# A deeper lead for the split of turned probability tiles in a fused attention and expert layer

## The chip, the cores and the metric

The kernel runs on one core of a Trainium2 chip. The metric is device time in microseconds (us) of one execution. A verdict of faster or slower needs a difference of over 2%.

## The reference

`x` is 2048 tokens by 256. The layer is attention and then a mixture of experts, each between two layer normalisations with a residual. Only the attention is touched by the change:

```python
x = L0_attn_x                                     # (1, 2048, 256)
# _L0_attn_ref, 16 heads of 128; w = codes * repeat(scales, 32)
q = _mxfp4_matmul(x, wq_codes, wq_scales) + bq    # the same for k and v
scores = jnp.einsum('bqhd,bkhd->bhqk', q, k) / jnp.sqrt(jnp.float32(HEAD_DIM))
attn = jax.nn.softmax(scores, axis=-1)            # 2048 x 2048 per head
out = jnp.einsum('bhqk,bkhd->bqhd', attn, v).reshape(B, S, NUM_HEADS * HEAD_DIM)
return _mxfp4_matmul(out, wo_codes, wo_scales) + bo
...
x = x + _layernorm(_L0_attn_ref(_layernorm(x, axis=-1), ...), axis=-1)
x = x + _layernorm(_L0_ffn_ref(_layernorm(x, axis=-1), ...), axis=-1)   # router, 8 experts, top 2
```

## The kernel before

Every float32 product is made of three products of a reduced float32 type (fp32r): each operand is split in a high part (the rounded copy) and a low part (operand minus high part), and hi x hi, hi x lo and lo x hi are summed (`product3`, lines 488 to 490). So each tile of probabilities needs a copy, which ScalarE (ACT) makes, and a subtraction, which GpSimd (POOL) makes.

The attention goes head by head (16), and in a head by chunks of 512 queries (4, index j), so there are 64 chunks. A chunk has 16 key positions of 128 keys and, at the same time, four row tiles of 128 queries (index r). Body (h, j) of the loop does two things interleaved: scores, maxima and exponentials of the *next* chunk (row tile r, in two halves g of 1024 keys), and the value products of the chunk that is under way. Positions 4r to 4r+3 belong to row tile r. "Step r" below is the time from the start of the first exponential of row tile r to the start of the next row tile's; a chunk is steps 0, 1, 2, 3.

The way of a probability: TensorE (PE) makes a half row tile of scores in `ps_s` (`scores`; three pairs of banks), VectorE (DVE) takes its maximum (L1000) and the shift (L1006), ACT the exponential (`exps`, L791), DVE turns it in blocks of 32 x 32 (`turn`, L1013), the DMA queue of SP brings the blocks of 1024 keys (group g) in place with 16 transfers (`turn_blocks`, L301) once the value products of the chunk before have used up the same group of `pT`, ACT copies a tile of 128 keys to `pT_hi` (`probs_hi`, L802), POOL subtracts in place (`probs_lo`, L393), and PE multiplies it with the values into `ps_a` (`weighted_values`). `pT_hi` is a ring of RING = 4 tiles: copy k waits until product k-4 is done.

The order on each engine is written out by hand and runs in order. At position p PE does the value product of key p - PV_LAG (12), ACT and POOL do copy and subtraction of key p - HI_LAG (10); a negative key is one of the chunk before. Around them, in step order:

- PE, row tile 3: scores (3,0), products 12 and 13, scores (3,1), the projection of queries (`q_proj`, which waits for `out_lo`), products 14 and 15. Row tile 0: products 0 and 1, scores (0,0), product 2, output projection, scores (0,1), product 3. In row tiles 1 and 2: scores (r,0), product 4r, product 4r+1, scores (r,1), products 4r+2 and 4r+3, with other projections between.
- ACT, each row tile: copies at 4r, 4r+1, 4r+2, exponential (r,0), copy at 4r+3, exponential (r,1). In row tile 3 `out_hi` stands behind the copy at 12, `q_hi` behind the copy at 14 and ahead of the exponential. At j = 3 the four copies of the next head's keys (`k_hi`) come before position 0.
- DVE, each row tile: maximum (r,0), turn (r-1,1), other work (`add_out`, L1040, in r = 0 and 1; `out_lo`, L1017, in r = 3), maximum (r,1), shift, turn (r,0).
- POOL: the weights of a head are unpacked between subtractions: keys at j = 0 and output at j = 1, both ahead of position 8; queries at j = 2 and values at j = 3, both ahead of position 0.
- SP: the 16 transfers of group 0, the 16 of group 1, and weight loads between; the query weights are loaded behind group 1 of body j = 1.

Of the kernel before, what the change touches and what calls it, by code (L numbers as in the profile page):

```python
# [8 lines left out]
def sandwich_layer(nc, x, wq, sq, bq, wk, sk, bk, wv, sv, bv, wo, so, bo, wr, wg, wu, wd, out):  # L9
# [35 lines left out]
    PAIRS = 3  # L45
    USES = TPC * NG2
    PV_LAG = 12
    HI_LAG = 10
    LOADS = Q4 * Q4 * 16
    CHUNKS = H * NCH  # L50

# [1 line left out]
    with ctx:  # L53
# [147 lines left out]
        def key_at(h, j, pos, lag):  # L201

            if pos >= lag:
                return (h, j, pos - lag) if has(h, j) else None
            if not has(h, j, -1):
                return None
            return ((h, j - 1) if j else (h - 1, NCH - 1)) + (pos + KT - lag,)
# [149 lines left out]
        def _(pool):  # L357
# [8 lines left out]
            def weights(k, h, codes=codes, scales=scales):  # L366

                wait(pool, w_loaded[k], 16 * (NG + 1) * (h + 1))

                if not isinstance(h, int) or h > 0:  # L370
                    if k == "o":
                        wait(pool, "oproj_ready", 2 * NCH * h)
                        wait(pool, "vb_ready", h)
                    else:
                        wait(pool, {"k": "k_lo", "v": "v_ready", "q": "q_lo"}[k], NCH * h)
                pool.tensor_tensor(w_hi[k][:, :, :], codes[:, :, :], scales[:, :, :], ALU.mult)\
                    .then_inc(w_hi_done[k], 1)
                col = {"o": "v", "k": "k", "q": "q", "v": None}[k]
                if col:
                    pool.tensor_copy(bias_now[col][:, :], bias_all[col][:, bass.ds(h, 1)])  # L380
                wait(pool, w_hi_done[k], h + 1)
                pool.tensor_tensor(codes[:, :, :], codes[:, :, :], scales[:, :, :], ALU.mult)\  # L382
                    .then_inc(w_scaled[k], 1)
                wait(pool, w_scaled[k], h + 1)
                pool.tensor_tensor(w_lo[k][:, :, :], codes[:, :, :], full(w_hi[k][:, :, :]), ALU.subtract)\
                    .then_inc(w_ready[k], 1)
# [14 lines left out]
            def body(h):  # L401
                before, last = isinstance(h, int) and h < 0, isinstance(h, int) and h == H - 1
                after = isinstance(h, int) and h == H
                for j in chunks_of(h):
                    for pos in range(KT):
                        if not before and not after:
# [6 lines left out]
                            if j == 3 and pos == 0 and not last:  # L413
                                weights("v", h + 1)
                        key = key_at(h, j, pos, HI_LAG)
                        if key:
# [347 lines left out]
        def _(act):  # L764
# [74 lines left out]
            def body(h):  # L839
                for j in chunks_of(h):  # L840
# [5 lines left out]
                    def key(pos):  # L846

                        at = key_at(h, j, pos, HI_LAG)
                        if at:
# [422 lines left out]
```

## Time and profile before

| | |
|---|---|
| median of 3 runs | 2824.37 us (2823.85 to 2857.05) |
| the profiled execution's own time | 2834.33 us |
| its span, first to last instruction | 2832.5 us |
| busy: PE, DVE, POOL, ACT | 81%, 61%, 55%, 49% of the span |
| mean granted TensorE clock | 0.943 |
| value part, first to last ScalarE copy (L802) | 94.2 to 2549.6 us |

A row of the timeline has the start of a group of instructions in us from the start of the span, its length, the engine, the line, the operation and its tiles, and in brackets the idle time of the engine before it and what ended that. Matmuls are pipelined: a value product is recorded as three matmuls of about 0.4 us, which start 0.23 us apart at full clock.

### The profile page before, as it was taken

To read this page: it belongs to the slowest core of one execution; us is meant where nothing else is said; L and a number is where in the kernel's file an instruction comes from. 1 tells how busy PE (TensorE), PEld (TensorE's weight loads), DVE (VectorE), ACT (ScalarE), POOL (GpSimd) and SP (SyncE) were. 2 spreads that over 40 slices of the span, in tenths; PEclk is the share of its full clock that TensorE was granted. 3 is DMA by queue.
4 is the path that set the end of the run, shared out by engine and by line. 5 is a ranking of instruction groups with operands and counts; after the bars stand their busy time and mean duration, and the time that the engine had idled before them with its cause. 6 is when DMAs were issued, how large, how long until landed. Compare 5 with 4: busy or idle time off the path is not lost.

```text
span 2832.5 us, 36223 instructions
## 1 busy us (share of the span) xinstructions
PE 2300.4 (81%) x10540; PEld 1812.0 (64%) x10540; DVE 1730.0 (61%) x2335; ACT 1389.5 (49%) x2492; POOL 1546.7 (55%) x1376
## 2 busy tenths in 40 slices
PE   4878787878788887878787878878787878855998
PEld 3667575756667666757575666657566657644876
DVE  4666666657566666666675756666666657645443
ACT  2454454545454555555454545544554545433332
POOL 1455556656565555565565656555556655554433
PEclk8999999989999999999999999999999999977999
DMA  4445454445454454555454645445455455470000
GB/s 75 112 109 118 105 126 112 112 107 134 102 125 109 111 126 105 117 126 118 105 121 110 135 103 124 113 108 117 105 126 120 112 116 120 113 180 11 8 8 15
DMA packets 152845, 298.68 MB, mean 105 GB/s; under 512 B 44896, under 2 KB 87264, under 8 KB 152800
## 3 DMA queue, kind: packets, MB, share of 16 engines
q1 hardware_dynamic: 152800, 298.11, 46.0%
q8 instruction: 24, 0.39, 0.1%
q14 instruction: 21, 0.17, 0.0%
HBM read 27.43 MB, written 2.10 MB: 10 GB/s over the span
## 4 chain that ended last, share of the span: by engine, by line
issue 41%; POOL 37%; PE 13%; DVE 4%; SPq 3%; DMA 2%; ACT 1%; POOLq 1%; ACTq 0%; DVEq 0%
POOL pT L393 33%; PE ps_s L488 2%; PE ps_s L489 2%; PE ps_s L490 2%; SPq L301 2%; POOL codes L382 1%; DVE part_max L1000 1%; DMA acc<-in_L_attn_bo 1%; PE ps_a L488 1%; PE ps_a L747 1%; DVE probs L1013 1%; PE ps_a L490 1%; PE ps_a L489 1%; PE ps_a L749 1%; PE ps_a L750 1%
## 5 line engine op out<-in xcount | busy, mean ns | idle before, releaser
L393 POOL TENSOR_TENSOR pT<-pT,pT_hi 128x512 fp32r<-128x512 f32 x1024 | 1298.4, 1289 | 975.5 <-ACT pT_hi L802 974.5
L791 ACT ACTIVATE probs<-ps_s,shift 128x1024 f32<-128x1024 f32 x512 | 569.2, 1112 | 777.6 <-DVE shift L1006 777.6
L488 PE MATMUL ps_a<-pT_hi,v_hi 128*128 128x512 f32 x1024 | 449.7, 439 | 408.3 <-POOL pT L393 408.2
L1000 DVE TENSOR_REDUCE part_max<-ps_s 128x1 f32<-128x1024 f32 x512 | 619.2, 1209 | 262.3 <-PE ps_s L490 261.2
L1013 DVE STREAM_TRANSPOSE probs<-probs 128x1024 f32<-128x1024 f32 x512 | 632.2, 1235 | 195.5 <-ACT probs L791 195.5
L802 ACT ACTIVATE pT_hi<-pT 128x512 fp32r<-128x512 f32 x1024 | 606.1, 626 | 76.1 <-DMA pT<-probs 55.1
L488 PEld LDWEIGHTS ps_a<-pT_hi,v_hi 128*128 128x128 f32 x1024 | 196.5, 192 | 559.6 <-POOL pT L393 526.4
L488 PE MATMUL ps_s<-kT_hi,qT_hi 128*128 128x512 f32 x1024 | 419.1, 409 | 9.1 <-ACT probs L791 6.6
L489 PE MATMUL ps_s<-kT_lo,qT_hi 128*128 128x512 f32 x1024 | 416.4, 407 | 0.0
L490 PE MATMUL ps_s<-kT_hi,qT_lo 128*128 128x512 f32 x1024 | 413.1, 403 | 0.0
L489 PE MATMUL ps_a<-pT,v_hi 128*128 128x512 f32 x1024 | 409.0, 399 | 0.0
L490 PE MATMUL ps_a<-pT_hi,v_lo 128*128 128x512 f32 x1024 | 408.6, 399 | 0.0
L488 PEld LDWEIGHTS ps_s<-kT_hi,qT_hi 128*128 128x128 f32 x1024 | 202.6, 198 | 55.2 <-ACT probs L791 8.6
L490 PEld LDWEIGHTS ps_s<-kT_hi,qT_lo 128*128 128x128 f32 x1024 | 201.5, 197 | 46.6
L489 PEld LDWEIGHTS ps_s<-kT_lo,qT_hi 128*128 128x128 f32 x1024 | 201.8, 197 | 42.2
L490 PEld LDWEIGHTS ps_a<-pT_hi,v_lo 128*128 128x128 f32 x1024 | 196.3, 192 | 44.8
L489 PEld LDWEIGHTS ps_a<-pT,v_hi 128*128 128x128 f32 x1024 | 197.4, 193 | 26.0
L1040 DVE SCALAR_TENSOR_TENSOR acc<-ps_a,rinv,acc 128x256 f32<-128x256 f32 x256 | 107.9, 462 | 136.0 <-PE ps_a L490 136.0
L488 PE MATMUL ps_a<-w_v_hi,xT_hi 128*128 128x128 f32 x512 | 146.2, 286 | 34.7 <-DVE oT_lo L1017 32.9
L1061 DVE TENSOR_TENSOR v_lo<-ps_a,v_hi 128x512 fp32r<-128x512 f32 x64 | 44.2, 691 | 176.0 <-ACT v_hi L830 176.0
L490 PE MATMUL ps_a<-w_v_hi,xT_lo 128*128 128x128 f32 x512 | 148.6, 290 | 0.0
L489 PE MATMUL ps_a<-w_v_lo,xT_hi 128*128 128x128 f32 x512 | 148.3, 290 | 0.0
(159 smaller groups left out, 2915.9 us busy)
## 6 DMA issues: line engine op xcount, KB each, us to landing
pT<-probs SPq DMA_DIRECT2D x2048, 128.0 KB, 2.4
probs<-in_L_attn_x SPq DMA_DIRECT2D x4, 512.0 KB, 5.3
codes<-in_L_attn_wk_codes SPq DMA_DIRECT2D x16, 128.0 KB, 2.2
scales<-in_L_attn_wk_scales SPq DMA_DIRECT2D x64, 32.0 KB, 2.8
acc<-in_L_attn_bo SPq DMA_DIRECT2D x1, 2048.0 KB, 31.2
codes<-in_L_attn_wo_codes SPq DMA_DIRECT2D x16, 128.0 KB, 2.1
scales<-in_L_attn_wo_scales SPq DMA_DIRECT2D x64, 32.0 KB, 1.8
x<-in_L_attn_x SPq DMA_DIRECT2D x4, 512.0 KB, 7.5
```

What stands on the lines that cost most here:

```text
L301: sp.dma_start(full(pT[32 * b:32 * (b + 1), g, i, :, :]).rearrange("p t q -> p (t q)"), blocks(j, g)[32 * i:32 * (i + 1), b].rearrange("p ...
L382: pool.tensor_tensor(codes[:, :, :], codes[:, :, :], scales[:, :, :], ALU.mult)\
L393: pool.tensor_tensor(tile, full(tile), full(pT_hi[:, k % RING, :]).rearrange("p (i q) -> p i q", i=Q4), ALU.subtract).then_inc(sm["p_lo_do ...
L488: nc.tensor.matmul(dst, lhs_hi, rhs_hi, start=first, stop=False)
L489: nc.tensor.matmul(dst, lhs_hi, rhs_lo, start=False, stop=False)
L490: return nc.tensor.matmul(dst, lhs_lo, rhs_hi, start=False, stop=last)
L791: nc.scalar.activation(out, src, ACT.Exp, bias=shift[:, j % 2, r:r + 1], scale=SCALE, accum_out=sums[:, j % 2, r, g:g + 1])\
L802: nc.scalar.activation(pT_hi[:, k % RING, :].rearrange("p (i q) -> p i q", i=Q4), full(pT[:, g, :, t, :]), ACT.Copy).then_inc(sm["p_hi_don ...
L1000: V.tensor_reduce(part_max[:, j % 2, r, g:g + 1], ps_s[:, pair_of(j, NG2 * r + g), :], AX.X, ALU.max)\
L1013: V.transpose(tile, tile).then_inc(sm["p_turned"], 1)
L1040: ins = V.scalar_tensor_tensor(acc[:, t, :], ps_a[:, j % 2, a * D:(a + 1) * D], rinv[:, jp % 2, 2 * i + a:2 * i + a + 1], acc[:, t, :], AL ...
L1061: V.tensor_tensor(v_lo[:, rows, :].rearrange("p a d -> p (a d)"), ps_a[:, bank, :], full(v_hi[:, rows, :]).rearrange("p a d -> p (a d)"), ...
```

## The change

Copies (ACT) and subtractions (POOL) of the turned tiles are done at position p for key p - 8 instead of p - 10. PE's products stay at p - 12, so they are led by four positions in place of two. The ring of four tiles stays.

```diff
     PV_LAG = 12
-    HI_LAG = 10
+    HI_LAG = 8
     LOADS = Q4 * Q4 * 16
```

The instruction order of PE, DVE and SP is the same. On ScalarE, body j = 1 of head 0, from row tile 2 (L802 is a copy, L791 an exponential, L810 `out_hi`; the brackets name the semaphores waited for, `pT_loaded0` is the landing of group 0, `pv_done` the value products). Before:

```order
L802 ACTIVATE pT_hi<-pT 128x512 [waits pv_done] x2
L802 ACTIVATE pT_hi<-pT 128x512 [waits pv_done,pT_loaded0]
L791 ACTIVATE probs,sums<-ps_s,shift 128x8x4x32 [waits shift_ready]
L802 ACTIVATE pT_hi<-pT 128x512 [waits pv_done]
L791 ACTIVATE probs,sums<-ps_s,shift 128x8x4x32 [waits shift_ready]
L802 ACTIVATE pT_hi<-pT 128x512 [waits pv_done]
L810 ACTIVATE oT_hi<-ps_a 128x4x4x32 [waits pv_done]
```

Changed:

```order
L802 ACTIVATE pT_hi<-pT 128x512 [waits pv_done,pT_loaded0]
L802 ACTIVATE pT_hi<-pT 128x512 [waits pv_done] x2
L791 ACTIVATE probs,sums<-ps_s,shift 128x8x4x32 [waits shift_ready]
L802 ACTIVATE pT_hi<-pT 128x512 [waits pv_done]
L791 ACTIVATE probs,sums<-ps_s,shift 128x8x4x32 [waits shift_ready]
L802 ACTIVATE pT_hi<-pT 128x512 [waits pv_done]
L810 ACTIVATE oT_hi<-ps_a 128x4x4x32 [waits pv_done]
```

The kinds of instructions keep their places; the copy that waits for the group's landing is the first of three ahead of the exponential, not the last.

On GpSimd, head 0, from its first subtraction (L393; L376 to L385 unpack weights: `w_o` at j = 1, `w_q` at j = 2). Before:

```order
L393 TENSOR_TENSOR pT<-pT,pT_hi 128x4x128 [waits p_hi_done] x14
L376 TENSOR_TENSOR w_o_hi<-codes,scales 128x256 [waits w_o_loaded]
L380 COPY bias_now_v<-bias_v 128x1
L382 TENSOR_TENSOR codes<-codes,scales 128x256 [waits w_o_hi_done]
L385 TENSOR_TENSOR w_o_lo<-codes,w_o_hi 128x256 [waits w_o_scaled]
L393 TENSOR_TENSOR pT<-pT,pT_hi 128x4x128 [waits p_hi_done] x8
L376 TENSOR_TENSOR w_q_hi<-codes,scales 128x256 [waits q_lo,w_q_loaded]
```

Changed:

```order
L393 TENSOR_TENSOR pT<-pT,pT_hi 128x4x128 [waits p_hi_done] x16
L376 TENSOR_TENSOR w_o_hi<-codes,scales 128x256 [waits w_o_loaded]
L380 COPY bias_now_v<-bias_v 128x1
L382 TENSOR_TENSOR codes<-codes,scales 128x256 [waits w_o_hi_done]
L385 TENSOR_TENSOR w_o_lo<-codes,w_o_hi 128x256 [waits w_o_scaled]
L393 TENSOR_TENSOR pT<-pT,pT_hi 128x4x128 [waits p_hi_done] x8
L376 TENSOR_TENSOR w_q_hi<-codes,scales 128x256 [waits q_lo,w_q_loaded]
```

Two more tiles are subtracted ahead of each unpacking of weights: ahead of the query weights 24 tiles (a whole chunk and half the next) and not 22.

## Rows read from the trace of the kernel before

**Rows 1.** The page's costliest groups: line, engine, operation, busy and mean ns, idle before.

```profile
L393 POOL TENSOR_TENSOR pT<-pT,pT_hi 128x512 fp32r<-128x512 f32 x1024 | 1298.4, 1289 | 975.5 <-ACT pT_hi L802 974.5
...
L488 PE MATMUL ps_a<-pT_hi,v_hi 128*128 128x512 f32 x1024 | 449.7, 439 | 408.3 <-POOL pT L393 408.2
```

**Rows 2.** Timeline of ACT, a plain chunk (j = 3): exponentials, one copy, q_hi.

```profile
1283.21 1.12 ACT L791 ACTIVATE probs<-ps_s,shift 128x1024 f32<-128x1024 f32 x1 [5.05 <-DVE shift L1006]
...
1290.22 1.12 ACT L791 ACTIVATE probs<-ps_s,shift 128x1024 f32<-128x1024 f32 x1 [2.62 <-DVE shift L1006]
...
1294.28 0.63 ACT L802 ACTIVATE pT_hi<-pT 128x512 fp32r<-128x512 f32 x1 [0.20 <-DMA pT<-probs]
...
1297.23 1.12 ACT L791 ACTIVATE probs<-ps_s,shift 128x1024 f32<-128x1024 f32 x1 [2.31 <-DVE shift L1006]
...
1304.31 0.69 ACT L816 ACTIVATE qT_hi<-ps_a,bias_now_q 128x512 fp32r<-128x512 f32 x1 [2.21 <-PE ps_a L490]
1304.89 1.11 ACT L791 ACTIVATE probs<-ps_s,shift 128x1024 f32<-128x1024 f32 x1
...
1315.02 1.11 ACT L791 ACTIVATE probs<-ps_s,shift 128x1024 f32<-128x1024 f32 x1 [5.12 <-DVE shift L1006]
```

**Rows 3.** Timeline of PE in the same chunk, value products and q_proj.

```profile
1293.35 0.50 PE L488 MATMUL ps_a<-pT_hi,v_hi 128*128 128x512 f32 x1 [1.09 <-POOL pT L393]
...
1302.60 0.51 PE L488 MATMUL ps_a<-xT_hi,w_q_hi 128*128 128x512 f32 x1
...
1304.10 0.40 PE L488 MATMUL ps_a<-pT_hi,v_hi 128*128 128x512 f32 x1
...
1308.01 0.50 PE L488 MATMUL ps_a<-pT_hi,v_hi 128*128 128x512 f32 x1 [1.65 <-POOL pT L393]
```

**Rows 4.** Timeline of DVE in the same chunk.

```profile
1287.88 0.83 DVE L1040 SCALAR_TENSOR_TENSOR acc<-ps_a,rinv,acc 128x256 f32<-128x256 f32 x2
...
1291.45 1.25 DVE L1013 STREAM_TRANSPOSE probs<-probs 128x1024 f32<-128x1024 f32 x1 [1.27 <-ACT probs L791]
...
1295.72 1.22 DVE L1000 TENSOR_REDUCE part_max<-ps_s 128x1 f32<-128x1024 f32 x1 [0.77 <-PE ps_s L490]
1296.98 0.21 DVE L1006 TENSOR_SCALAR shift<-part_max 128x1 f32<-128x1 f32 x1
...
1301.89 0.65 DVE L1017 TENSOR_TENSOR oT_lo<-ps_a,oT_hi 128x512 fp32r<-128x512 f32 x1
```

**Rows 5.** Timeline of SP's queue: group 0 of that chunk.

```profile
1282.29 10.03 SPq L301 DMA_DIRECT2D pT<-probs  x16
```

**Rows 6.** Timeline of ACT, chunk j = 1, row tiles 2 and 3, then row tile 0.

```profile
1219.10 1.11 ACT L791 ACTIVATE probs<-ps_s,shift 128x1024 f32<-128x1024 f32 x1 [2.48 <-DVE shift L1006]
...
1229.32 1.11 ACT L791 ACTIVATE probs<-ps_s,shift 128x1024 f32<-128x1024 f32 x1
...
1246.81 1.12 ACT L791 ACTIVATE probs<-ps_s,shift 128x1024 f32<-128x1024 f32 x1 [12.71 <-DVE shift L1006]
```

**Rows 7.** Timelines of SP's queue, POOL and PE around the query weights.

```profile
1221.42 10.03 SPq L301 DMA_DIRECT2D pT<-probs  x16
...
1236.92 0.72 POOL L376 TENSOR_TENSOR w_q_hi<-codes,scales 128x256 fp32r<-128x256 f32 x1 [4.53 <-DMA scales<-in_L_attn_wq_scales]
...
1239.21 3.74 POOL L393 TENSOR_TENSOR pT<-pT,pT_hi 128x512 fp32r<-128x512 f32 x3
...
1240.52 0.79 PE L488 MATMUL ps_a<-pT_hi,v_hi 128*128 128x512 f32 x1 [5.74 <-POOL pT L393]
```

**Rows 8.** Windows: length, busy of PE, PEld, DVE, ACT, POOL, granted clock, DMA.

```profile
1240.00:1244.00 4.00, 3.48 (x11) 3.09 (x12) 0.51 (x2) 0.00 (x0) 2.94 (x3) 0.50 0.00 0
```

**Rows 9.** Timeline of ACT, row tile 3 of chunk j = 2.

```profile
1268.84 1.11 ACT L791 ACTIVATE probs<-ps_s,shift 128x1024 f32<-128x1024 f32 x1
```

**Rows 10.** Timeline of ACT, row tile 3 of chunk j = 0, then row tile 0.

```profile
1348.43 1.11 ACT L791 ACTIVATE probs<-ps_s,shift 128x1024 f32<-128x1024 f32 x1
...
1358.49 1.12 ACT L791 ACTIVATE probs<-ps_s,shift 128x1024 f32<-128x1024 f32 x1 [5.69 <-DVE shift L1006]
```

## The prediction

> **What bounds the kernel now.** I read the page's costliest groups first, then the timeline of one head engine by engine. In the groups, TensorE (PE) stands idle 408.2 us in all before value products, waiting for POOL's subtraction, and POOL stands idle 974.5 us waiting for ACT's copy [rows 1]. So POOL is not short of time; the copies come late. The timeline says why. ACT's exponentials open every step, and in a plain chunk (j = 3) they start at 1283.21, 1290.22, 1297.23, 1304.89 and 1315.02: steps of 7.01, 7.01, 7.66 and 10.13, together 31.81 us [rows 2]. The copy at position 4r+3 stands behind the exponential (r,0), and with a lead of two it feeds the product at 4(r+1)+1, which stands ahead of the scores (r+1,1), whose maximum the next exponential needs. That is a closed loop: exponential, copy, subtraction, product, scores, maximum, exponential. It shows as PE's stalls of 1.09 and 1.65 us behind POOL [rows 3] and as DVE's 0.77 us of idle time behind PE in step 1 [rows 4].
>
> **The change.** No instruction is added or removed; 1024 copies and 1024 subtractions come two positions earlier. The copy behind exponential (r,0) now feeds the product at 4(r+1)+3, behind the scores (r+1,1), so the loop is opened. What is late next, step by step:
>
> Step 1. Without the stall, DVE is next: an exponential, 1.27 us until the turn may start [rows 4], then turn, maximum, turn, maximum, shift with nothing between. In step 1 that chain holds 0.77 us of idle time, so it comes to 7.01 - 0.77 = 6.24 us. PE needs less: two half tiles of scores and four products are 24 matmuls, 0.23 us apart, 5.5 us. Gain 0.8 us in chunks 1, 2 and 3; in chunk 0 value projections fill PE, and I take none. Step 0 has `add_out` (0.83 us [rows 4]) in the same chain: 6.24 + 0.83 = 7.07 against 7.01 now, so DVE bounds it already. Gain nil.
>
> Step 2 gets worse. The copy at 14 now takes a tile whose ring place is free only when the product at position 14 itself is done, and on PE that product stands behind `q_proj`. `q_proj` starts at 1302.60 when `out_lo` (1301.89 + 0.65) is there, the product at 14 at 1304.10 [rows 3, 4]. `q_hi` followed the projection at 1304.31 [rows 2]. It will follow copy 14: 1304.10, two matmul starts of 0.23 and the last matmul of 0.40 give 1304.96, plus a copy slot of 0.52 (the estimate is a copy's 0.63 less the overlap of about 0.1 us with its successor) gives 1305.5. So `q_hi` and the exponential (3,0) come 1.2 us later in every chunk. Loss 1.2 us x 4. In chunk 1 the step is 10.22 us now [rows 6], with stalls behind POOL unpacking `w_o`; the two tiles more of lead cover them, and it becomes 7.66 + 1.2 = 8.9. Net gain there 1.3.
>
> Step 3. The three products at 15, 0 and 1 no longer wait. From `q_proj`'s end PE has four products, scores, a product, an output projection and scores, some 6.9 us, which falls short of DVE's chain with an `add_out`, 7.0 us from the exponential (3,0). 10.13 [rows 2] and 10.06 [rows 10] become 7.0: gain 3.1 in chunks 3 and 0. In chunk 2 (14.37 us, 1268.84 to 1283.21 [rows 9, 2]) the next head's keys are projected in between; their chain does not move, only the stall behind it does, one of the kind of [rows 3]. I estimate the end of the step 0.9 us earlier (just under the 1.09 us there), its start 1.2 later, gain 2.1.
>
> Step 3 of chunk 1 is the large one: 17.49 us, 1229.32 to 1246.81 [rows 6]. POOL reaches the query weights at position 0 of body 2 and waits for them until 1236.92; subtractions go on at 1239.21, PE had stood 5.74 us, and then ran at the half clock: 0.50 granted, the 1.2 GHz level [rows 7, 8]. Now POOL has finished keys 4 to 7 of that chunk before it stops, which feed PE's products 0 to 3, both half tiles of scores, and so the next exponential. This step becomes 7.0 too, gain 10.5. The weights arrive no earlier, though: POOL resumes 17.8 us after SP started group 1 (1221.42 to 1239.21 [rows 7]), so the first tile is subtracted 1.3 us later [rows 1], 19.0 us after group 1's start, which is about exponential (2,0). PE wants it 16.3 us after: exponential (0,0) at 15.9 (8.9 + 7.0), its scores ended 1.7 before, a product (0.7) and scores (1.4) behind them. PE stands some 2.7 us. From 19.0 it has two products and an output projection (2.1), scores (1.4) and the 1.7 to the exponential: 24.2, against 15.9 + 7.0 = 22.9. Loss 1.2, rounded down.
>
> The sum per head is 3 x 0.8 - 3 x 1.2 + 1.3 + 2 x 3.1 + 2.1 + 10.5 - 1.2 = 17.7 us. With 15.5 heads (the first and last chunks lack parts of it) that is 274 us. The profiled execution took 2834 us, so 2560; it stands 10 us over the median, so I say **2550 us**.
>
> **The clock after the new stall.** The row at hand is a stall of 5.74 us with a half clock behind it; stalls of 1.09 and 1.65 us do not come with a slower product behind them [rows 3]. A stall of 2.7 us is between, nearest to the second; I take full clock. The other end: about 4 us at half clock, 2 us of work lost, 16 times, +32 us, and as much again where it falls twice. The Trainium skill, "TensorE: Matmul & The Clock Gate", section on the HAM clock gate, speaks for the slower end: the default state is throttled and activity releases it. By that reading the sum would be 2582 to 2614.
>
> **Transfers.** The first copy of each group is due earlier, and it stands ahead of an exponential. For group 0 SP starts 0.92 us before the exponential (0,0) (1282.29 against 1283.21), and the copy that waited for the landing starts at 1294.28, 11.99 us after [rows 5, 2]. So the copies at 8, 9, 10 can start 11.07 us after exponential (0,0) and take 1.6: 12.7, while the exponential (2,0) is due at 7.01 + 6.24 = 13.25. It holds by 0.6 us. Group 1 starts when product 11 is done, about exponential (2,0), and lands 12 us on, with 15.9 us to the exponential that needs it (8.9 + 7.0). I cost both at nothing. If the cover is gone, each late us is paid in full.
>
> **Rivals.** (1) *The transfers become the bound.* For: the margin of 0.6 us. Against: their start moves with PE's products, which get earlier too. If group 0 comes 2.4 us late for every chunk (as far as the copies at 8 and 9 and a stretch of SP's weight loads could put it), 64 x 2.4 = 154 us: about 2700.
> (2) *The ring takes the gain and the loss stays: slower.* The copy of key k waits for product k - 4, and with HI_LAG 8 these are at the same position. ACT is tied to PE there, ahead of the exponential. If PE still waits for POOL as often, because copies cannot run ahead of the ring, nothing is gained and the 1.2 us of step 2 is paid 64 times: +77 us, 2901 on the median. It decides where copy 4r+2 ends after the shift is ready. After scores (r,1) PE does the product at 4r+2 (0.69 us, 0.2 us to the end of the last matmul, copy slot 0.5: 1.4 us), while maximum and shift take from 1295.72 to 1297.23, 1.5 us, and 0.2 us of drain [rows 4, 2]: it holds by 0.3 us in steps 0 and 1. A busy POOL could use that up.
> (3) *The waits only move.* The stall behind the query weights moves from position 2 to position 4 in full length, and the rest is DVE's: 2824.
> (4) *The clock* as above: 2550 + 50 = 2600.
>
> **Numbers.** Forecast 0.66, clock 0.06, transfers 0.11: faster 0.83. Waits that move: 0.07 within 2%. Ring: 0.10 slower by over 2%. (Two per cent, 56 us, is what a measurement of this kernel can tell from no change.) The range begins at 2480, where step 2 loses nothing (64 x 1.2 = 77 us, 2473), and goes to 2730, past the transfers' case; outside are the last two cases.
>
> **What would show it.** In the new profile: idle time of PE behind POOL under 100 us; steps of a plain chunk of 7.0, 6.2, 8.9 and 7.0 us; the copy ahead of `q_hi` waiting for PE; the first exponential of body 2 about 7 us behind its predecessor, and PE idle for about 2.7 us at the first product of the row tile after it; ACT's waits for a landing late in the gap before an exponential that waits for the shift. I am wrong if ACT goes from a landing or a product directly to the exponential (0,0), (1,0) or (2,0) with the shift long ready, or if PE still stands behind POOL for hundreds of us.

## The result: 8.7% faster

The changed kernel takes 2588.22 us (median of 4 runs, 2584.68 to 2592.03) against 2828.9 us before on the same chip; the ratio is 0.9131, with a 95% interval of 0.9068 to 0.9194. The prediction was 2550 us in a range of 2480 to 2730. The profiled execution has a span of 2584.8 us against 2832.5.

### The profile page after: what moved, and what is told of

Its sections match the earlier page's. It is cut to its first block, busy times and chain, and to the rows that moved or that the text cites. A ratio compares the mean times of both kernels' runs of the same rounds, so it can differ in the third digit from the quotient of the medians.

```text
span 2584.8 us, 36223 instructions
## 1 busy us (share of the span) xinstructions
PE 2257.8 (87%) x10540; PEld 1810.7 (70%) x10540; DVE 1709.4 (66%) x2335; ACT 1406.0 (54%) x2492; POOL 1548.0 (60%) x1376
## 4 chain that ended last, share of the span: by engine, by line
issue 39%; POOL 37%; PE 14%; DVE 4%; SPq 2%; DMA 2%; ACT 1%; POOLq 1%; DVEq 0%; ACTq 0%
POOL pT L393 33%; PE ps_s L488 3%; PE ps_s L490 2%; PE ps_s L489 2%; POOL codes L382 2%; DVE probs L1013 1%; SPq L301 1%; DVE part_max L1000 1%; DMA acc<-in_L_attn_bo 1%; PE ps_a L747 1%; PE ps_a L488 1%; PE ps_a L490 1%; PE ps_a L489 1%; PE ps_a L749 1%; PE ps_a L750 1%
## 5 line engine op out<-in xcount | busy, mean ns | idle before, releaser
L393 POOL TENSOR_TENSOR pT<-pT,pT_hi 128x512 fp32r<-128x512 f32 x1024 | 1299.3, 1291 | 781.3 <-ACT pT_hi L802 781.2
L802 ACT ACTIVATE pT_hi<-pT 128x512 fp32r<-128x512 f32 x1024 | 616.8, 627 | 443.3 <-PE ps_a L490 367.3
L791 ACT ACTIVATE probs<-ps_s,shift 128x1024 f32<-128x1024 f32 x512 | 569.2, 1112 | 337.6 <-DVE shift L1006 337.6
L488 PE MATMUL ps_a<-pT_hi,v_hi 128*128 128x512 f32 x1024 | 421.0, 411 | 75.0 <-POOL pT L393 75.0
L489 PE MATMUL ps_s<-kT_lo,qT_hi 128*128 128x512 f32 x1024 | 410.3, 401 | 0.0
L1047 DVE SCALAR_TENSOR_TENSOR qT_lo<-ps_a,bias_now_q,qT_hi 128x512 fp32r<-128x512 f32 x64 | 48.0, 751 | 177.8 <-ACT qT_hi L816 157.5
L488 PEld LDWEIGHTS ps_a<-w_v_hi,xT_hi 128*128 128x128 f32 x512 | 107.6, 210 | 69.9 <-issue 45.0
```

The lines of the kernel that those rows point to most:

```text
L393: pool.tensor_tensor(tile, full(tile), full(pT_hi[:, k % RING, :]).rearrange("p (i q) -> p i q", i=Q4), ALU.subtract).then_inc(sm["p_lo_do ...
L488: nc.tensor.matmul(dst, lhs_hi, rhs_hi, start=first, stop=False)
L489: nc.tensor.matmul(dst, lhs_hi, rhs_lo, start=False, stop=False)
L791: nc.scalar.activation(out, src, ACT.Exp, bias=shift[:, j % 2, r:r + 1], scale=SCALE, accum_out=sums[:, j % 2, r, g:g + 1])\
L802: nc.scalar.activation(pT_hi[:, k % RING, :].rearrange("p (i q) -> p i q", i=Q4), full(pT[:, g, :, t, :]), ACT.Copy).then_inc(sm["p_hi_don ...
L1047: V.scalar_tensor_tensor(qT_lo[:, :], ps_a[:, (j + 1) % 2, :], bias_now["q"][:, :], full(qT_hi[:, :]), ALU.add, ALU.subtract).then_inc(sm[ ...
```

## The profile after

The page's groups that answer to [rows 1], and one that was small before: line, engine, operation, busy and mean ns, idle before.

```profile
L393 POOL TENSOR_TENSOR pT<-pT,pT_hi 128x512 fp32r<-128x512 f32 x1024 | 1299.3, 1291 | 781.3 <-ACT pT_hi L802 781.2
L802 ACT ACTIVATE pT_hi<-pT 128x512 fp32r<-128x512 f32 x1024 | 616.8, 627 | 443.3 <-PE ps_a L490 367.3
...
L488 PE MATMUL ps_a<-pT_hi,v_hi 128*128 128x512 f32 x1024 | 421.0, 411 | 75.0 <-POOL pT L393 75.0
```

PE's idle time behind POOL has gone from 408.2 to 75.0 us. In its place ACT waits 367.3 us for PE before copies: that is the ring, and it costs only where an exponential is queued behind the copy and the shift is ready.

A plain chunk (j = 3), timeline of ACT, to set beside [rows 2]:

```profile
1293.19 1.12 ACT L791 ACTIVATE probs<-ps_s,shift 128x1024 f32<-128x1024 f32 x1 [3.31 <-DVE shift L1006]
...
1300.10 1.12 ACT L791 ACTIVATE probs<-ps_s,shift 128x1024 f32<-128x1024 f32 x1 [1.95 <-DVE shift L1006]
...
1304.00 1.67 ACT L802 ACTIVATE pT_hi<-pT 128x512 fp32r<-128x512 f32 x3 [1.08 <-DMA pT<-probs]
1306.23 1.11 ACT L791 ACTIVATE probs<-ps_s,shift 128x1024 f32<-128x1024 f32 x1 [0.55 <-DVE shift L1006]
...
1313.97 0.63 ACT L802 ACTIVATE pT_hi<-pT 128x512 fp32r<-128x512 f32 x1 [3.40 <-PE ps_a L490]
1314.51 0.67 ACT L816 ACTIVATE qT_hi<-ps_a,bias_now_q 128x512 fp32r<-128x512 f32 x1
1315.08 1.11 ACT L791 ACTIVATE probs<-ps_s,shift 128x1024 f32<-128x1024 f32 x1
...
1322.42 1.12 ACT L791 ACTIVATE probs<-ps_s,shift 128x1024 f32<-128x1024 f32 x1 [2.96 <-DVE shift L1006]
```

The steps are 6.91, 6.13, 8.85 and 7.34 us, where 7.0, 6.2, 8.9 and 7.0 were forecast. Three copies start together at 1304.00, after a wait for the landing, and the exponential behind them still waits 0.55 us for the shift: the transfers are covered, by little. At 1313.97 the copy at 14 waits 3.40 us for PE with `q_hi` and the exponential queued behind it: the new wait of step 2.

DVE in step 1 of the same chunk, to set beside [rows 4]:

```profile
1301.34 1.25 DVE L1013 STREAM_TRANSPOSE probs<-probs 128x1024 f32<-128x1024 f32 x1 [1.27 <-ACT probs L791]
...
1303.62 1.22 DVE L1013 STREAM_TRANSPOSE probs<-probs 128x1024 f32<-128x1024 f32 x1
1304.76 1.19 DVE L1000 TENSOR_REDUCE part_max<-ps_s 128x1 f32<-128x1024 f32 x1
1305.98 0.21 DVE L1006 TENSOR_SCALAR shift<-part_max 128x1 f32<-128x1 f32 x1
```

No idle time stands before the second maximum any more: DVE bounds steps 0 and 1.

Around the query weights, to set beside [rows 7]; timelines of SP's queue, POOL and PE:

```profile
1239.23 10.03 SPq L301 DMA_DIRECT2D pT<-probs  x16
...
1254.84 0.74 POOL L376 TENSOR_TENSOR w_q_hi<-codes,scales 128x256 fp32r<-128x256 f32 x1 [1.76 <-DMA scales<-in_L_attn_wq_scales]
...
1257.17 1.27 POOL L393 TENSOR_TENSOR pT<-pT,pT_hi 128x512 fp32r<-128x512 f32 x1
...
1258.49 0.50 PE L488 MATMUL ps_a<-pT_hi,v_hi 128*128 128x512 f32 x1 [1.00 <-POOL pT L393]
```

The way from group 1's start to POOL's next subtraction is 17.9 us (17.8 before), but PE stands 1.00 us in place of 5.74, and its next matmul takes 0.50 us in place of 0.79. In heads 1 to 14 the stall is 0.89 to 1.73 us, but for one head of 2.07 us, in which the clock falls after all and step 0 is 9.12 us:

```profile
1815.80 0.79 PE L488 MATMUL ps_a<-pT_hi,v_hi 128*128 128x512 f32 x1 [2.07 <-POOL pT L393]
```

All heads, for which I took the start of the first exponential of each row tile from ACT's timeline, heads 1 to 14, means in us:

| | step 0 | step 1 | step 2 | step 3 |
|---|---|---|---|---|
| chunk 0 before / after | 7.02 / 6.91 | 10.91 / 10.99 | 16.36 / 18.31 | 10.04 / 7.26 |
| chunk 1 | 7.02 / 6.91 | 7.02 / 6.13 | 9.20 / 8.93 | 18.79 / 7.25 |
| chunk 2 | 7.02 / 7.11 | 7.31 / 7.09 | 7.66 / 9.26 | 14.39 / 13.14 |
| chunk 3 | 7.01 / 6.91 | 7.02 / 6.14 | 7.66 / 9.33 | 10.12 / 7.48 |

A head is 154.55 us before and 139.17 after; 16 times the difference is 246 us, and the spans differ by 247.7.

## The experiments

Times are medians of 4 runs; the kernel before stands beside each at 2827 to 2830 us. Steps are means over heads 1 to 14, as in the table above, where no single head is named. A lower clock in a step is the mean granted clock of that step's own window.

**The halves.** The change acts on two engines. Alone on POOL, it only moves each unpacking of weights two tiles back; alone on ACT, it opens the loop and leaves the unpacking where it was.

In the POOL block of the kernel before (`HI_LAG = 10`), for POOL's half:

```diff
-                        key = key_at(h, j, pos, HI_LAG)
+                        key = key_at(h, j, pos, 8)
```

In the POOL block of the changed kernel (`HI_LAG = 8`), for ACT's half:

```diff
-                        key = key_at(h, j, pos, HI_LAG)
+                        key = key_at(h, j, pos, 10)
```

> Only POOL's half of the change: subtractions and the unpacking of weights are placed for key p - 8, while ACT copies for key p - 10 as before, so the only thing that moves is that each unpacking stands two tiles later among the subtractions. Theory (two separate mechanisms, the loop through the copy behind the exponential and the stall behind the query weights): the loop stays, steps of a plain chunk remain 7.0, 7.0, 7.7, 10.1 us; the step 3 of chunk 1, 18.8 us on average before, falls to about 10.1 us and the one before it from 9.2 to about 7.7; about 9.5 us per head, 145 us in all: 2680 us. Rival (all of the gain is the loop through ACT's copies): within 1% of the kernel before, 2825 us. Rival (all of the gain is the weights): 2590 us.

> Only ACT's half: copies for key p - 8, while the subtractions and the unpacking of weights stand as before (key p - 10), so unpacking stands two tiles earlier than in the changed kernel. Theory: plain chunks as in the changed kernel (6.9, 6.1, 8.9 or a little more, 7.3 us); after the query weights PE waits at product 2 again, ahead of the scores that the next exponential needs, so step 3 of chunk 1 is about 13 us in place of 7.3; 6 us per head, 95 us in all over the changed kernel: 2685 us. Rival (all of the gain is the loop): as the changed kernel, 2590 us. Rival (all of it is the weights): 2825 us.

Measured: POOL's half 2700.04 us (ratio 0.9525, 0.9476 to 0.9575), ACT's half 2710.35 us (0.9574, 0.9532 to 0.9617); 2680 and 2685 were expected. In POOL's half steps 0 to 3 of a plain chunk stay at 7.01, 7.01, 7.66 and 10.13, while step 3 of chunk 1 is 10.05 and step 2 of it 8.29. Timeline of ACT there:

```profile
1231.45 1.11 ACT L791 ACTIVATE probs<-ps_s,shift 128x1024 f32<-128x1024 f32 x1
...
1241.58 1.11 ACT L791 ACTIVATE probs<-ps_s,shift 128x1024 f32<-128x1024 f32 x1 [5.14 <-DVE shift L1006]
```

In ACT's half a plain chunk has the steps of the changed kernel (6.91, 6.19, 9.54, 7.71), and step 3 of chunk 1 is 15.49. The stall is back on PE, about as long as it was (4.82 to 7.46 us in heads 1 to 14, 5.74 to 8.29 before):

```profile
1182.76 0.80 PE L488 MATMUL ps_a<-pT_hi,v_hi 128*128 128x512 f32 x1 [6.26 <-POOL pT L393]
```

The halves save 128.7 and 118.4 us, 247 together, and the whole change 240.7. So there are two mechanisms of about equal size that hardly touch each other, and both single-cause rivals are out.

**Product 14 ahead of the query projection.** In the changed kernel copy 14 waits for product 14, which stands behind `q_proj`.

```diff
+                        if r == 3:
+                            key(TPC * r + 2)
                         if r == 3 and has(h, j, 2):
                             q_proj(*after)
-                        if r:
+                        if r in (1, 2):
                             key(TPC * r + 2)
```

> The changed kernel with PE's product 14 ahead of the query projection and not behind it. Theory (copy 14 waits for product 14, and through q_hi this holds back the exponential (3,0)): step 2 falls from 8.9 to 9.3 us to about 7.7 us in chunks 1, 2 and 3, PE's idle time ahead of the projection is filled, 1.4 us four times a head: 2500 us. Rival (step 2 is long because DVE's out_lo and the projection come when they come, or because of the half clock): within 1% of the changed kernel, 2590 us.

Measured: 2543.81 us (0.8994, 0.8954 to 0.9035). Step 2 is 7.66, 7.72 and 7.66 us in chunks 3, 1 and 2. Timeline of ACT, one such step:

```profile
1282.07 1.12 ACT L793 ACTIVATE probs<-ps_s,shift 128x1024 f32<-128x1024 f32 x1 [0.58 <-DVE shift L1008]
...
1289.14 0.69 ACT L818 ACTIVATE qT_hi<-ps_a,bias_now_q 128x512 fp32r<-128x512 f32 x1 [2.21 <-PE ps_a L490]
1289.72 1.11 ACT L793 ACTIVATE probs<-ps_s,shift 128x1024 f32<-128x1024 f32 x1
```

`q_hi` waits for the projection alone, by the same 2.21 us as in [rows 2]; ACT's wait for PE before copies falls from 367.3 to 221.9 us. The cause of the longer step 2 is shown. The gain was half of what I expected (44 us, not 88): step 0 of chunk 2 rose from 7.11 to 9.10 us, because all but the query weights came earlier.

**Query weights two positions later, on top of that.**

```diff
-                            if j == 2 and pos == 0 and not last:
+                            if j == 2 and pos == 2 and not last:
                                 weights("q", h + 1)
```

> Product 14 ahead of the query projection, and the query weights unpacked two positions later (position 2 of body 2). Theory: in the run with product 14 first, step 0 of chunk 2 was 9.1 us on average in place of 6.9, because everything but the arrival of the weights came 1.4 us earlier; two more tiles ahead of the unpacking take this away: 2 us per head, 2544 - 32 = 2512 us. Rival (that step is long for another reason, the half clock or the transfers): no change from 2544 us.

Measured: 2527.06 us (0.8938, 0.8904 to 0.8972). Step 0 of chunk 2 is 6.91 in every head, as expected. But 17 us are gained, not 32: step 1 of chunk 0 went from 11.21 to 12.59 us and step 1 of chunk 2 from 7.04 to 7.56, while step 2 of chunk 0 fell by 0.9. The clock accounts for both losses. Step 1 of chunk 0 is 10.64 to 10.68 us in the four heads with a granted clock of 1.00, and 13.81 to 13.87 us in the seven with 0.75 or 0.76; with product 14 first alone, only two heads of 14 had that. Step 1 of chunk 2 is 6.94 or 6.95 us at 1.00, and 7.67 to 7.95 at 0.78 or 0.79. Two heads of this run (windows over the step: length, busy of PE, PEld, DVE, ACT, POOL, granted clock, DMA):

```profile
621.17:631.84 10.67, 10.67 (x72) 9.63 (x72) 6.23 (x7) 6.02 (x10) 6.45 (x9) 1.00 0.27 62
1159.90:1173.74 13.84, 13.84 (x72) 12.22 (x72) 6.35 (x7) 6.02 (x10) 6.44 (x9) 0.75 0.21 47
```

PE has the same 72 matmuls and is busy throughout in both. Why more heads lose the clock in this kernel stays open.

**A lead of three.** Copies and subtractions for key p - 9.

```diff
-    HI_LAG = 8
+    HI_LAG = 9
```

> HI_LAG 9: a lead of three. Theory: the copy behind the exponential (r,0) now feeds the product at 4(r+1)+2, still behind the scores (r+1,1), so the loop is open and step 1 stays at 6.1 us; the copy at 14 waits for product 13, which stands ahead of the query projection, so step 2 returns to about 7.7 us in place of 8.9 to 9.3 (1.4 us less, four times a head); the query weights are unpacked one tile earlier, PE stands about 3 us at product 3 and step 0 of chunk 2 becomes about 10 us. Together 2.4 us per head less than the changed kernel: 2550 us. Rival (a lead of less than four does not open the loop): step 1 back at 7.0 us and 2650 us or more.

Measured: 2674.28 us (0.9445, 0.9399 to 0.949), a miss by 124 us. Steps 1 and 2 of a plain chunk are as expected: 6.91, 6.17, 7.65 and 8.15 us, so the loop is open and step 2 is repaired. But step 3 gives part of it back: 8.07 to 8.15 us in chunks 0, 1 and 3 against 7.25 to 7.48 in the changed kernel, and 13.93 against 13.14 in chunk 2, 3.1 us per head that the expectation put at nothing. Step 0 of chunk 2 is 12.92 us, not 10, and step 2 of chunk 1 9.61. The stall at product 3 was not 3 us but 4.79 to 6.87, and the half clock followed, which I had not costed. Timeline of PE, and windows behind it:

```profile
1165.79 0.73 PE L488 MATMUL ps_a<-pT_hi,v_hi 128*128 128x512 f32 x1 [5.06 <-POOL pT L393]
```

```profile
1166.00:1170.00 4.00, 4.00 (x11) 3.10 (x12) 0.26 (x1) 0.63 (x1) 4.00 (x4) 0.59 0.36 80
```

**A lead of three, with the weights' places kept.** All four unpackings one position later (9, 9, 1, 1).

```diff
-                            if j == 2 and pos == 0 and not last:
+                            if j == 2 and pos == 1 and not last:
                                 weights("q", h + 1)
```

> Lead of three, with each unpacking of weights one position later, so that it stands behind the same tile as in the changed kernel. Theory (what the lead of three lost against expectation, 12.9 us in step 0 of chunk 2 and 9.6 in step 2 of chunk 1, is POOL's unpacking alone): those steps return to about 7.1 and 7.7 us, the rest stays, 136.8 us per head against 139.2 in the changed kernel: 2550 us. Rival (a lead of three does not give POOL enough time): 2640 us or more, with PE idle behind POOL for over 150 us.

Measured: 2599.7 us (0.9192, 0.9166 to 0.9218). Seventy-five of the 124 us were the weights' places; 50 remain. Step 0 of chunk 2 is 9.74 us on average (6.91 to 11.84). In a head where it is 11.16, PE stands 2.80 us, and half clock follows:

```profile
1269.66 0.79 PE L488 MATMUL ps_a<-pT_hi,v_hi 128*128 128x512 f32 x1 [2.80 <-POOL pT L393]
```

```profile
1272.00:1276.00 4.00, 4.00 (x12) 3.23 (x12) 0.88 (x2) 0.63 (x1) 3.83 (x4) 0.52 0.91 208
```

Most of the 50 us are in this step, 2.6 us per head more than the 7.1 expected. PE's idle time behind POOL is 131.3 us in all. The first account held for 75 us, the rival's 2640 did not come either: a lead of three is long enough for the loop in step 1, and too short where POOL stops for weights.

Step 3 of a plain chunk is 8.16 us here too. Timeline of DVE behind the exponential (3,0), which starts at 1326.83:

```profile
1330.37 1.22 DVE L1000 TENSOR_REDUCE part_max<-ps_s 128x1 f32<-128x1024 f32 x1 [1.07 <-PE ps_s L490]
```

That idle time is 0.23 us in the changed kernel. The exponential comes earlier, but the products behind `q_proj` still stand ahead of the next scores on PE, which now bounds the step. So of the 1.2 us that step 2 gets back at full clock, step 3 takes 0.8. Product 14 moved ahead of the projection has both short, 7.66 and 7.49 us. Against the changed kernel (2588.22 us) this run is within 1%.

**Transfers held back.** SP waits for one value product more before group 0.

```diff
-                wait(sp, "pv_done", KT * (m - 1) + GT * (g + 1))
+                wait(sp, "pv_done", KT * (m - 1) + GT * (g + 1) + (1 if g == 0 else 0))
```

> The changed kernel, with the transfers of group 0 held back by one value product more (SP waits for product 4 of the running order and not product 3), some 2.1 us later. Theory: the copies at 8, 9 and 10 stand ahead of the exponential (2,0) with 0.44 us to spare, so step 1 grows by about 1.6 us in the three chunks without value projections and not in the fourth: 48 x 1.6 = 77 us, 2665 us. Rival (the spare time is larger, since PE runs ahead of DVE): within 1% of 2590 us. Rival (a landing is paid in full in all chunks): 2720 us.

Measured: 2642.4 us (0.9346, 0.9318 to 0.9374), 54 us over the changed kernel. Step 1 is 7.60, 7.62 and 7.89 us in chunks 3, 1 and 2: 1.5 us more in the first two and 0.8 in the third. In chunk 0, where nothing was expected, it is 12.12 in place of 10.99, again with the lower clock in more heads. That would be 4.9 us per head or 78 us; 54 came because step 2 was shorter in return, by 0.4 to 0.65 us in chunks 3, 2 and 0 (8.83 to 8.92 us in every head of chunks 3 and 2). Timeline of ACT; the exponential behind the copies has no wait of its own any more:

```profile
1186.95 1.11 ACT L791 ACTIVATE probs<-ps_s,shift 128x1024 f32<-128x1024 f32 x1 [1.95 <-DVE shift L1006]
1192.89 1.67 ACT L802 ACTIVATE pT_hi<-pT 128x512 fp32r<-128x512 f32 x3 [3.11 <-DMA pT<-probs]
...
1194.46 1.10 ACT L791 ACTIVATE probs<-ps_s,shift 128x1024 f32<-128x1024 f32 x1
```

So the first rival's mechanism exists and its margin is about half a microsecond; it did not decide, because the margin was there.

**Useless matmuls.** Step 2 of chunk 0 became 1.95 us longer, where the ring accounts for 1.2. The changed kernel has a wait of 2.33 us for `out_lo` there, and a half-clock stretch behind it in every head (18.28 to 18.36 us, granted clock 0.81). Windows of the changed kernel:

```profile
1206.00:1210.00 4.00, 1.71 (x8) 1.08 (x6) 3.90 (x4) 2.36 (x5) 3.23 (x3) 1.00 0.87 197
1210.00:1214.00 4.00, 3.96 (x25) 3.99 (x26) 0.00 (x0) 0.00 (x0) 0.27 (x1) 0.70 0.93 213
1214.00:1218.00 4.00, 4.00 (x10) 3.13 (x11) 1.96 (x3) 0.60 (x1) 0.00 (x0) 0.50 0.67 167
```

```diff
+            def keep_busy(h, j):
+                wait(pe, "p_ready", USES * (NCH * h + j) + USES - PAIRS)
+                for _ in range(9):
+                    nc.tensor.matmul(ps_s[:, pair_of(j, USES - 1), 0:CH], qT_hi[:, 3 * P:4 * P],
+                                     kT_hi[:, 0:CH], start=True, stop=True)
...
                         if r == 3 and j == 0 and has(h, j):
+                            keep_busy(*nxt)
                             v_proj(h, 3)
```

> The changed kernel with nine extra matmuls (128x512, results overwritten by the scores behind them) once per head in chunk 0, ahead of the projection of values 3, where PE waits 2.3 us for out_lo. The extra matmuls take about 2.1 us. Theory (step 2 of chunk 0, 18.3 us, holds a stretch at half clock that follows this idle time): granted clock stays at full in it, the step falls by about 2 us or more, 30 to 40 us in all: 2550 us. Rival (the half clock is not the cause, or the extra work is paid): 2588 us or more.

Measured: 2544.69 us (0.9008, 0.8979 to 0.9037): 144 matmuls that compute nothing make the kernel 43 us faster. The step is 15.46 us in place of 18.31 (15.44 to 15.48 in all heads), and the same stretch runs at full clock:

```profile
1185.00:1189.00 4.00, 3.71 (x18) 2.81 (x16) 3.68 (x4) 2.15 (x5) 3.23 (x3) 1.00 0.91 207
1189.00:1193.00 4.00, 4.00 (x30) 3.52 (x29) 0.56 (x1) 0.60 (x1) 0.09 (x1) 1.00 0.89 205
1193.00:1197.00 4.00, 3.94 (x18) 3.15 (x18) 1.75 (x4) 1.43 (x3) 0.72 (x1) 1.00 0.66 163
```

This also measures the ring by itself. The kernel before has a wait of 2.20 us at the same place, and its step 2 of chunk 0 ranges from 14.25 to 18.71 us, at granted clocks of 1.00 to 0.73. A head at full clock, window over the step:

```profile
1486.40:1500.65 14.25, 12.00 (x71) 9.82 (x71) 7.03 (x10) 6.65 (x12) 5.25 (x5) 1.00 0.66 149
```

At full clock before and after, the step goes from 14.25 to 15.46: 1.2 us for the ring, as predicted. The half clock cost 2.1 us on average before and 2.85 in the changed kernel. The mean granted clock goes from 0.952 to 0.972. The Trainium skill, "TensorE: Matmul & The Clock Gate", section on the HAM clock gate, says that the throttled state is the default and activity releases it; by that, filling the wait keeps the clock, and the trace agrees (1.00 against 0.50 to 0.70).

**All repairs.** First the three together, then the scores (3,1) moved ahead of the projection of values 3, so that needed work fills the wait.

```diff
+                        if has(h, j, 1):
+                            scores(*nxt, r, 1)
                         if r == 3 and j == 0 and has(h, j):
                             v_proj(h, 3)
-                        if has(h, j, 1):
-                            scores(*nxt, r, 1)
```

> All three repairs: product 14 ahead of the query projection, query weights two positions later, nine useless matmuls where PE waits for out_lo in chunk 0. Theory (three separate causes, which add up): 2527 - 1.5 us per head or more for the clock (step 2 of chunk 0, 16.3 us, to about 14.4 or less): 2500 us, 11.5% under the kernel before. Rival (product 14 first has already taken what the clock gave): 2527 us.

> Product 14 first and query weights two positions later, and in chunk 0 the scores (3,1) stand ahead of the projection of values 3 and not behind it, so that PE does needed work while it waits for out_lo, in place of useless matmuls. Theory: 1.4 of the 2.3 us of idle time are filled and the stretch at half clock goes; the scores no longer stand between the projection of values and the query projection, where PE now waits for v_lo, so it is worth less than the useless matmuls or as much: 2500 to 2510 us. Rival (the wait for v_lo brings the half clock back): 2527 us or more.

Measured: 2492.18 us (0.881, 0.8788 to 0.8832) and 2484.94 us (0.8779, 0.8757 to 0.8801). Step 2 of chunk 0 is 14.59 and 14.49 us. The intervals overlap a little, so the two are not told apart, but the second needs no extra work. It beats the kernel before by 12.2%, measured beside it, and the changed kernel by 4.0% (2484.94 / 2588.22, not measured side by side; the ratios to the kernel before give 3.9%).

A ring with more tiles, which would take the copies' wait away without moving a product, was not tried.

## Why the prediction was right

**What bounded the kernel.** The loop through the copy behind the exponential, and POOL's stop for the query weights, are both shown, by the halves.

**Steps 0 and 1.** Step 1 was to fall by 0.8 us in three chunks; it fell by 0.9 in chunks 1 and 3, and by 0.2 in chunk 2. There I forgot the two operations for the value bias in DVE's chain (L1067 and L1074, 0.36 and 0.38 us), which bound that step as `add_out` bounds step 0. Step 0 was to stay, and fell by 0.1.

**Step 2.** The mechanism was right, as the run with product 14 first shows, and where the clock stays up so is the size: 8.85 us in the chunk above is 7.66 + 1.19. The mean was mis-sized: +1.7, +1.6 and +1.95 us in chunks 3, 2 and 0, in place of 1.2. In 7 of 14 heads in chunk 3 and 4 of 14 in chunk 2 the half clock comes in behind PE's wait for `out_lo`, and the step is 9.63 to 10.42 us. A step 2 of 9.72 us (from 1167.47), timeline of PE and the window behind it:

```profile
1172.84 0.50 PE L488 MATMUL ps_a<-xT_hi,w_q_hi 128*128 128x512 f32 x1 [1.97 <-DVE oT_lo L1017]
```

```profile
1174.00:1176.00 2.00, 2.00 (x7) 1.53 (x6) 0.17 (x1) 0.00 (x0) 0.00 (x0) 0.51 0.89 203
```

The same wait stands in the chunk of 8.85 us, and there the window behind it has the full clock:

```profile
1311.60 0.50 PE L488 MATMUL ps_a<-xT_hi,w_q_hi 128*128 128x512 f32 x1 [1.97 <-DVE oT_lo L1017]
```

```profile
1312.00:1314.00 2.00, 2.00 (x11) 1.63 (x9) 0.89 (x2) 0.03 (x1) 0.20 (x1) 1.00 0.91 207
```

In chunk 1 I took the 10.22 us of one head for the rule and put the excess down to POOL alone. The step was 8.62 to 8.67 us in nine heads at full clock and 10.11 to 10.23 in five with a granted clock of 0.83, on average 9.20, and so the gain was 0.3 and not 1.3. Step 2 in all was to cost 3.6 - 1.3 = 2.3 us per head and cost 4.95. That is 41 us over 15.5 heads, more than the whole difference between the 274 us forecast and the 241 us saved; the other terms together made up a little, since the loss of 1.2 us costed for step 0 hardly came.

**Step 3.** 3.1 us were forecast in chunks 3 and 0, 2.6 and 2.8 came; in the plain chunk above DVE still waits 0.23 us for the scores of row tile 0. In chunk 2 it was 1.25 and not 2.1. In chunk 1 the large term was 10.5; 11.5 came, since other heads had lost more than the one read.

**The query weights.** They were to leave a stall of 2.7 us and a loss of 1.2 us in step 0; the stall is 1.2 us on average, and the loss 0.1. I let group 1 start at the exponential (2,0). It starts 1.82 us ahead of it (1239.23 against 1241.05), because PE, freed from POOL, runs ahead of DVE, and the weights are queued behind that group. The transfers of group 0 were costed at nothing by a margin of 0.6 us: the exponential (2,0) still waits 0.41 to 0.56 us for the shift in chunks 1 and 3, and the run with the transfers held back shows the cost once that is used up.

**The rivals.** The ring did not take the gain: copies wait for PE 367 us, in the shadow of the shift, except in step 2. The clock fell behind the query weights in one head of 14, but for a reason I did not have: the stall was 1.2 us and not 2.7. Whether full clock was the right choice for 2.7 us the runs do not settle. In the lead of three with the weights' places kept it fell behind 2.80 us; in the kernel with useless matmuls a stall of 2.71 us at the same product went by at full clock:

```profile
285.88 0.50 PE L488 MATMUL ps_a<-pT_hi,v_hi 128*128 128x512 f32 x1 [2.71 <-POOL pT L393]
```

```profile
286.00:290.00 4.00, 4.00 (x21) 3.41 (x22) 2.81 (x5) 1.26 (x2) 4.00 (x4) 1.00 0.88 204
```

That this term did no harm was in part luck: the stall was costed too long, so the choice about the clock was hardly put to the test.

## What to carry to other kernels

When a producer two engines away is given more lead, ask three things: which product its copy feeds (ahead of or behind the work that releases the copy), which product its ring slot waits for and what stands before that in its queue, and what else stands in the producers' queues at that tile. Here the number of positions mattered less than these places: a lead of three was 3% slower than one of four until the unpacking of weights was moved with it, and then within 1%; moving one product over a projection was worth 44 us. Where steps are bounded in turn by different engines, ask also what the next step has when one step gets shorter: step 3 took back 0.8 of the 1.2 us that a lead of three gave step 2. Run each engine's half of such a change alone; a saving that looks like one mechanism can be two.

## What the runs showed that was not expected

A stretch at half clock followed single idle times of PE of 1.97, 2.07, 2.33, 2.80 and 5.06 us. Others of 1.97, 2.34 (chunk 0 of a head with the query weights two positions later) and 2.71 us went without, and behind the 2.20 us in chunk 0 of the kernel before the step was at full clock in 3 heads of 14 and below it in 11. So the length of one wait does not say whether the clock falls; what does is not shown. But idle time at PE can be charged beyond its length: 2.33 us of it, filled with useless matmuls, gave 2.85 us back per head. And a mean over heads can hide two levels: in step 1 of chunk 0, 10.6 and 13.8 us are the same work at a granted clock of 1.00 and 0.75.
